# Order of the conditioning chain and of the ScalarE copies in an adaLN, attention and GRU kernel

## The chip, the cores and the metric

One core of one Trainium2 chip runs the whole kernel. The metric is device time in microseconds (us), from one launch. The kernel before takes 487.22 us, the median of three runs (486.86 to 487.56).

## The reference, cut to what matters

The input x is 128 batches x 32 positions x 256 features, float32; cond is 128 x 256. The program computes three things one after another:

```python
# 1. conditioning: block attention over 8 blocks of 4 positions
block_repr = x.reshape(B, 8, 4, H).sum(axis=2)
keys = block_repr @ Wk.T
keys = keys / sqrt(mean(keys**2) + EPS) * rms_weight
attn = softmax(keys @ q)                          # q = cond[1], 8 weights per batch
proj = (attn @ block_repr) @ Wo.T                 # one row per batch
y = layernorm(x + proj) * gamma + beta            # proj is spread over the 32 positions
# 2. causal attention, 32 heads of 8 features, 32 positions, with ALiBi
q, k, v = split(y @ W_attn + b_attn)
x = x + softmax(mask(q @ k.T / sqrt(8)) + alibi) @ v @ W_proj + b_proj
# 3. GRU over 32 time steps (state starts at cond), then a 256 x 256 linear layer
x = x + gru(cond, x) @ (weight * scale).T + bias
```

## The kernel before, in words

**Tiles and groups.** A tile is 128 tokens, that is 4 batches of 32 positions. Four tiles make a group of 16 batches; there are 8 groups and 32 tiles. The main loop runs over groups g and, within one, over steps i = 0 to 3 (`tile_step(g, i)`, with n = 4g + i). Each engine has its own `tile_step`, and the order of the calls in it, written out by hand, is the order of the work on that engine. Semaphores order the engines among each other; an engine that waits holds up all that stands behind it. After the groups the GRU runs, 32 steps one after another (lines 1311 to 1332); the change doesn't touch it.

**What a step does for attention.** TensorE (`tile_step` at L1202) computes the scores of tile n + 1 (L1115), transposes the attention output of tile n - 1 (L1149), transposes the probabilities of tile n (L1128), projects the output of tile n - 1 (L1157), and multiplies probabilities by values for tile n (`probs_v`, L1139). VectorE normalises (L805, L809), applies the mask (L784), takes the row maxima (L792), subtracts the maximum from the first half of the scores (L798) and adds the residual (L821). GpSimd (POOL) subtracts it from the second half (L469). ScalarE takes the exponentials (L561) and copies results out of PSUM: the transposed probabilities and attention output (both L491, as `copy_out`).

**What is done for the next group.** In step 0 TensorE transposes y of group g + 1 (`transpose_y`, L1055) into ps_a, once ScalarE's `cond_out` has emptied it (L1051). ScalarE's `transpose_out` (L527) reads each of the two feature halves twice: as yT_r[0], rounded to the fp32r format, and as yT in full. GpSimd's `rest_of_y` (L443) subtracts them, which gives the low part yT_r[1]. `work_ahead` on TensorE then computes q in step 0 and k in step 1 (both L1066) and v in step 2 (L1075), each product as high x high, low x high, high x low; ScalarE writes them out in `q_chunk`, `k_chunk`, `v_half`. SyncE moves k and v by DMA into block-diagonal tiles (`load_k` L332, `save_v` L336, `load_v` L342).

**The conditioning chain for group g + 2.** In step 3 of the group before, TensorE multiplies the block sums by Wk and Wo (`block_products`, L1013), and ScalarE copies the product to kw_sb (`cond_out`, by L491). Then, in step 0: VectorE `cond_sums` (L699, L701, L704), GpSimd `inverse_rms` (the power -1/2, L436), VectorE `cond_scores` (L708), TensorE `cond_row` (L1025: the column of scores is turned into a row in ps_o). In step 1: VectorE `cond_shift` (L716, L718), ScalarE `cond_exp` (L512), VectorE `cond_normalise` (L723 to L727), TensorE `cond_col` (L1030), VectorE `select_blocks` (L734), TensorE `batch_proj` (L1036), ScalarE `round_proj`, VectorE `rest_of_proj` (L740), TensorE `spread_proj` (L1042). In step 2 VectorE adds the projection to x (L750) and takes the statistics (L758, L766), from which GpSimd makes the inverse deviation; in step 3 ScalarE's `normalise_tokens` (L519) makes y. This chain exists for groups g + 2 < 8, that is in the steps of groups 0 to 5.

Of the kernel before, what the change touches and what calls it, by code (L numbers as in the profile page):

```python
# [8 lines left out]
ACT = mybir.ActivationFunctionType  # L9
# [10 lines left out]
C = E // P  # L20
# [3 lines left out]
NG = B // GB  # L24
NT = B // TB
# [55 lines left out]
def adaln_attn_gru_ffn(nc, x_tok, x_feat, cond_t, wkwo, wqkv, wp, wih, whh, wf, vecs, rows, consts, v_dram, out):  # L81
    ctx = ExitStack()
    with ctx:
# [41 lines left out]
        vec = sb("vec", [P, NVEC])  # L125
# [287 lines left out]
        def _(pool):  # L413
# [20 lines left out]
            def inverse_rms(k):  # L434
                pool.wait_ge(c_mean, k + 1)
                nc.gpsimd.tensor_tensor(rinv[:, :], rinv[:, :], minus_half[:, 0:1], ALU.pow).then_inc(c_pow, 1)  # L436
# [36 lines left out]
            for g in range(NG):  # L473
                for i in range(GT):
                    n = GT * g + i
                    if i == 0 and g + 1 < NG:
                        rest_of_y(g + 1)
                    if i == 0 and g + 2 < NG:
                        inverse_rms(g + 2)
                    if n + 1 < NT:  # L480
                        softmax_shift(n + 1)
                    if i == 1 and g + 3 < NG:
                        block_sums(g + 3)
                    if i == 2 and g + 2 < NG:
                        inverse_std(g + 2)
# [3 lines left out]
        def _(act):  # L489
# [29 lines left out]
                    nc.scalar.activation(y[:, i, :], y[:, i, :], ACT.Identity, bias=centre[:, i:i + 1],  # L519
                                         scale=rstd[:, i:i + 1]).then_inc(y_done, 1)  # L520

            def transpose_out(k):

                for c in range(C):
                    act.wait_ge(yt_mm, C * k + c + 1)
                    for dst, out_sem in ((yT_r[0], yt_hi), (yT, yt_out)):
                        nc.scalar.activation(dst[:, c, :], ps_a[:, c * 512:(c + 1) * 512], ACT.Identity,  # L527
                                             bias=vec[:, V_BETA + c:V_BETA + c + 1],
                                             scale=vec[:, V_GAMMA + c:V_GAMMA + c + 1]).then_inc(out_sem, 1)

            def q_chunk(k, m):

# [50 lines left out]
            cond_out(1, ps_m[:, :])  # L583
            normalise_tokens(0)
            act.wait_ge(l_small, 3 * DMA)
            transpose_out(0)
            act.wait_ge(w_ready, 1)
            q_chunk(0, 0)
            q_chunk(0, 1)
# [10 lines left out]
            def tile_step(g, i):  # L600

                n = GT * g + i
                last_group = g + 1 == NG
                if i == 0 and not last_group:
                    transpose_out(g + 1)
                if i == 1 and g + 2 < NG:
                    cond_exp(g + 2)
                if n > 0:
                    attn_out(n - 1)
                probs_out(n)  # L610
                if i == 0 and not last_group:
                    q_chunk(g + 1, 0)
                    q_chunk(g + 1, 1)
                if i == 1 and not last_group:
                    k_chunk(g + 1, 0)
                    k_chunk(g + 1, 1)
                if i == 1 and g + 2 < NG:
                    round_proj(g + 2)
                if i == 2 and not last_group:
                    v_half(g + 1, 0)  # L620
                    v_half(g + 1, 1)
                if i == 3 and g + 2 < NG:
                    normalise_tokens(g + 2)
                if n + 1 < NT:
                    softmax_exp(n + 1, (n + 1) % 2)
                if i == 3 and g + 3 < NG:
                    cond_out(g + 3, ps_a[:, 0:512])
                if g == NG - 2 and i <= C:
                    if i == 0:
                        act.wait_ge(wqkv_lo, 3)  # L630
                        act.wait_ge(w_ready, 2)
                    if i < C:
                        copy_out(w_ih_r[0][:, i, :], w_ih[:, i, :]).then_inc(w_hi, 1)
                    else:
                        copy_out(w_f_r[0][:, :, :], w_f[:, :, :]).then_inc(w_hi, 1)
# [43 lines left out]
        def _(dve):  # L679
# [200 lines left out]
            def tile_step(g, i):  # L880

                n = GT * g + i
                norm_ahead = g + 2 < NG
                if n > 0:
                    normalise(n - 1)
                if norm_ahead and i == 1:
                    cond_shift(g + 2)
                if norm_ahead and i == 2:
                    add_proj(g + 2)
                if n + 1 < NT:  # L890
                    softmax_mask(n + 1, (n + 1) % 2)
                if norm_ahead and i == 0:
                    cond_sums(g + 2)
                if norm_ahead and i == 1:
                    cond_normalise(g + 2)
                if norm_ahead and i == 2:
                    token_stats(g + 2)
                if n + 1 < NT:
                    softmax_max(n + 1, (n + 1) % 2)
                if norm_ahead and i == 1:  # L900
                    select_blocks(g + 2)
                if n + 1 < NT:
                    softmax_shift(n + 1, (n + 1) % 2)
                if norm_ahead and i == 2:
                    mean_and_variance(g + 2)
                if norm_ahead and i == 0:
                    cond_scores(g + 2)
                if g == NG - 2 and 0 < i:
                    rest_of_gru_weights(i - 1)
                if n > 0:  # L910
                    residual(n - 1, (n - 1) // GT, (n - 1) % GT)
                if norm_ahead and i == 1:
                    rest_of_proj(g + 2)
# [95 lines left out]
        def _(pe):  # L1009
# [192 lines left out]
            def tile_step(g, i):  # L1202

                n = GT * g + i
                last_group, norm_ahead = g + 1 == NG, g + 2 < NG
                if i == 0 and not last_group:
                    transpose_y(g + 1, norm_ahead)
                if n + 1 < NT:
                    scores(n + 1, (n + 1) // GT, (n + 1) % GT)
                if n > 0:  # L1210
                    transpose_attn(n - 1)
                transpose_probs(n, n % 2, first=(n == 0))
                if n > 0:
                    project_out(n - 1)
                if norm_ahead and i == 1:
                    cond_col(g + 2)
                if i < 3 and not last_group:
                    work_ahead(g + 1, i, 0)
                    work_ahead(g + 1, i, 1)
                if norm_ahead and i == 0:  # L1220
                    cond_row(g + 2)
                if g + 3 < NG and i == 3:
                    pe.wait_ge(v_out, 2 * g + 4)
                    block_products(g + 3, ps_a[:, 0:512])
                if norm_ahead and i == 1:
                    pe.wait_ge(k_out, 2 * g + 3)
                    batch_proj(g + 2)
                probs_v(n, g, i)
                if norm_ahead and i == 1:
                    pe.wait_ge(k_out, 2 * g + 4)  # L1230
                    spread_proj(g + 2)

            for g in range(NG):
                for i in range(GT):
# [158 lines left out]
```

## Time and profile before

| | |
|---|---|
| median of 3 runs | 487.22 us |
| profiled execution | 486.86 us |
| its span, first to last instruction | 485.1 us |
| TensorE (PE) busy | 438.2 us, 90% |
| VectorE (DVE) busy | 343.6 us, 71% |
| ScalarE (ACT) busy | 241.1 us, 50% |
| GpSimd (POOL) busy | 108.4 us, 22% |

The busy time is the sum of an engine's instructions over the whole span. An engine that is busy for a small share can still end a wait of another, so the table alone doesn't say what a change of order is worth. PEld is TensorE's loading of weights, which runs beside its products. In rows of the timeline the first number is the start in us from the span's start, the second the time that the instruction, or the run of them, took. Instructions of one engine overlap there by some hundredths of a microsecond.

### The profile page before, as it was taken

What the parts mean: (1) busy time and instruction counts of PE and PEld (TensorE: products, weight loads), DVE (VectorE), ACT (ScalarE), POOL (GpSimd) and SP (SyncE); (2) the same over time, 40 slices, a digit from 0 to 9 for tenths busy, and PEclk for the clock granted to TensorE, in tenths of its full rate; (3) what the DMA queues carried; (4) which work ended last, traced back from release to release, by engine and by line L of the source; (5) the groups of instructions that cost most, each with busy time, mean ns of one, the idle gap of its engine ahead of it and who ended that gap; (6) DMA issues with size and microseconds to landing.
All of it is one profiled execution on the core that took longest, in us unless ns stands there. A gap on an engine that the chain in (4) does not pass through costs nothing.

```text
span 485.1 us, 13494 instructions
## 1 busy us (share of the span) xinstructions
PE 438.2 (90%) x5458; PEld 359.0 (74%) x5458; DVE 343.6 (71%) x1015; ACT 241.1 (50%) x561; POOL 108.4 (22%) x119
## 2 busy tenths in 40 slices
PE   7679789899898998998989786999999999999995
PEld 5247467667676785776767675979998999899984
DVE  3815388789787987888888885366677767676665
ACT  1252545756648457466486454444444444444342
POOL 7330334443334445333251221000000000000000
PEclk9759899999999999999999999999999999999999
DMA  8511411332503314123130220000100001010101
GB/s 302 228 43 35 143 44 34 89 104 64 155 20 92 111 41 129 64 74 95 29 95 20 62 66 3 1 2 1 43 23 24 22 24 45 0 45 2 43 23 65
DMA packets 34268, 30.36 MB, mean 63 GB/s; under 512 B 4128, under 2 KB 29344, under 8 KB 34208
## 3 DMA queue, kind: packets, MB, share of 16 engines
q1 hardware_dynamic: 34208, 29.51, 19.1%
q8 instruction: 43, 0.70, 0.6%
q14 instruction: 17, 0.14, 0.1%
HBM read 16.91 MB, written 8.39 MB: 52 GB/s over the span
## 4 chain that ended last, share of the span: by engine, by line
PE 68%; DVE 14%; issue 7%; ACT 5%; SPq 3%; DMA 2%; POOL 1%; DVEq 0%; ACTq 0%; POOLq 0%
PE ps_a L1066 7%; PE ps_s L1271 6%; PE ps_t L1271 6%; PE ps_o L1271 6%; PE ps_s L1243 5%; PE ps_s L1115 5%; PE ps_t L1243 4%; PE ps_a L1075 4%; PE ps_a L1243 4%; PE ps_m L1243 3%; PE ps_m L1157 3%; PE ps_o L1139 3%; PE ps_t L1128 3%; SPq L332 2%; PE ps_a L1013 2%
## 5 line engine op out<-in xcount | busy, mean ns | idle before, releaser
L469 POOL TENSOR_TENSOR sc<-masked,mx 128x512 f32<-128x512 f32 x32 | 46.2, 1445 | 123.8 <-DVE mx L792 123.8
L1066 PE MATMUL ps_a<-yT_r,w_qkv_r 128*128 128x512 f32 x192 | 51.5, 418 | 1.5 <-ACT yT_r L527 1.5
L784 DVE COPY_PREDICATED masked<-kst,ps_s 128x512 f32<-128x512 int32 x64 | 44.0, 734 | 9.7 <-PE ps_s L1115 6.3
L1066 PEld LDWEIGHTS ps_a<-yT_r,w_qkv_r 128*128 128x128 f32 x192 | 36.5, 198 | 10.4 <-issue 2.1
L561 ACT ACTIVATE sc<-sc 128x512 f32<-128x512 f32 x64 | 37.1, 622 | 7.6 <-DVE sc L798 6.2
L792 DVE TENSOR_REDUCE mx<-masked 128x16 f32<-128x512 f32 x64 | 40.4, 672 | 0.0
L647 ACT ACTIVATE zg<-ps_t,brz 128x128 f32<-128x128 f32 x64 | 20.0, 364 | 38.8 <-PE ps_t L1271 38.8
L929 DVE SCALAR_TENSOR_TENSOR rg<-ps_o,vec,rg 128x128 f32<-128x128 f32 x64 | 19.5, 346 | 27.3 <-PE ps_o L1271 23.4
L1157 PE MATMUL ps_m<-oT,w_p 128*128 128x128 f32 x256 | 35.4, 282 | 3.6 <-ACT oT L491 3.6
L491 ACT ACTIVATE pT<-ps_t 128x512 f32<-128x512 f32 x64 | 35.0, 599 | 4.2 <-PE ps_t L1128 3.5
L1115 PE MATMUL ps_s<-kbd,qn 64*32 64x256 f32 x1024 | 35.9, 390 | 0.7 <-DMA kbd<-kn 0.7
L1128 PE MATMUL ps_t<-kst,sc 128*128 128x128 f32 x256 | 35.4, 282 | 1.1 <-issue 1.1
L1271 PEld LDWEIGHTS ps_s<-hT,w_hh 128*128 128x128 f32 x256 | 33.1, 191 | 4.5 <-DVE hT L947 2.4
L1157 PEld LDWEIGHTS ps_m<-oT,w_p 128*128 128x128 f32 x256 | 31.7, 195 | 5.4 <-ACT oT L491 5.3
L1271 PE MATMUL ps_s<-hT,w_hh 128*128 128x128 f32 x256 | 34.2, 276 | 0.9 <-DVE hT L947 0.6
L1271 PE MATMUL ps_o<-hT,w_hh 128*128 128x128 f32 x256 | 33.8, 275 | 0.0
L1271 PE MATMUL ps_t<-hT,w_hh 128*128 128x128 f32 x256 | 33.8, 275 | 0.0
L1128 PEld LDWEIGHTS ps_t<-kst,sc 128*128 128x128 f32 x256 | 30.5, 147 | 2.4 <-issue 2.4
L647 ACT ACTIVATE rg<-ps_s,brz 128x128 f32<-128x128 f32 x64 | 20.0, 363 | 24.3 <-PE ps_s L1271 24.3
L1271 PEld LDWEIGHTS ps_t<-hT,w_hh 128*128 128x128 f32 x256 | 31.2, 192 | 0.1
L1271 PEld LDWEIGHTS ps_o<-hT,w_hh 128*128 128x128 f32 x256 | 31.2, 192 | 0.0
L491 ACT ACTIVATE h_r<-hT 128x256 fp32r<-128x256 f32 x32 | 13.4, 418 | 35.7 <-DVE hT L947 35.7
(116 smaller groups left out, 872.8 us busy)
## 6 DMA issues: line engine op xcount, KB each, us to landing
xf<-in_x_feat SPq DMA_DIRECT2D x8, 512.0 KB, 4.2
xg<-in_x_tok SPq DMA_DIRECT2D x8, 512.0 KB, 5.0
kbd<-kn SPq DMA_DIRECT2D x128, 32.0 KB
v_dram<-vn SPq DMA_DIRECT2D x16, 256.0 KB, 2.5
vbd<-v_dram SPq DMA_DIRECT2D x64, 64.0 KB, 2.0
out_feat<-ost SPq DMA_DIRECT2D x16, 256.0 KB, 2.0
w_qkv<-in_wqkv SPq DMA_DIRECT2D x1, 768.0 KB, 7.5
w_ih<-in_wih SPq DMA_DIRECT2D x1, 768.0 KB, 10.2
```

Of the source, the lines that this page charges most:

```text
L469: nc.gpsimd.tensor_tensor(shifted, kept, m.unsqueeze(2).to_broadcast([P, NH // 2, S]), ALU.subtract).then_inc(sc_sub[1], 1)
L491: return nc.scalar.activation(dst, src, ACT.Copy)
L561: nc.scalar.activation(part, part, ACT.Exp).then_inc(sc_exp, 1)
L647: nc.scalar.activation(dst[:, c, :], gate_part(gate, c, t), ACT.Sigmoid, bias=brz[:, b0 + c:b0 + c + 1]).then_inc(done, 1)
L784: nc.vector.copy_predicated(kept, keep.unsqueeze(1).to_broadcast([P, NH // 2, S]), ps_s[:, h * 512:(h + 1) * 512].rearrange("p (h k) -> p ...
L792: nc.vector.tensor_reduce(m, kept, axis=AX_X, op=ALU.max).then_inc(sc_max, 1)
L1066: last = nc.tensor.matmul(bank, w_qkv_r[a][:, c, first_col + m * P:first_col + (m + 1) * P], yT_r[b][:, c, :], start=(a == b == c == 0), s ...
L1115: last = nc.tensor.matmul(ps_s[b * S:(b + 1) * S, out_cols], qn[rows, g % 2, c, cols], kbd[rows, c, :, cols], start=True, stop=True, tile_ ...
L1128: last = nc.tensor.transpose(ps_t[:, col:col + P], sc[:, p, col:col + P], ident)
L1157: last = nc.tensor.matmul(ps_m[:, E + m * P:E + (m + 1) * P], w_p[:, c, m * P:(m + 1) * P], oT[:, c, :], start=(c == 0), stop=(c == C - 1))
L1243: last = nc.tensor.matmul(dst, w_r[a][:, c, col:col + P], rhs_r[b][:, c, :], start=first, stop=(c == C - 1 and a == 1), skip_group_check=True)
L1271: last = nc.tensor.matmul(dst, w_hh[:, c, col + m * P:col + (m + 1) * P], old[:, c, :], start=(which is None and c == 0 and m == 0), stop= ...
```

## The change

It reorders calls in the four `tile_step`s; no instruction is added or taken away except waits. GpSimd: `inverse_rms` goes ahead of `rest_of_y`. ScalarE: `transpose_out` is cut into its four copies, and the last of them goes behind `attn_out`; `cond_exp` moves from the beginning of step 1 to between the two copies of q in step 0; `cond_out` goes ahead of the exponentials of step 3. VectorE: in step 0, `cond_sums` goes ahead of the mask, `cond_scores` directly behind it, and `cond_shift` comes from step 1 to behind the subtraction of the maximum; in step 1, `cond_normalise` goes ahead of the mask and `select_blocks` ahead of the maxima. TensorE: `cond_row` goes ahead of the q products, `cond_col` ahead of the transposes of the probabilities; `probs_v` of step 0 now first waits for `c_sub`; `spread_proj` is written at the beginning of step 2 instead of the end of step 1.

```diff
--- before.py
+++ after.py
@@ -473,10 +473,10 @@
             for g in range(NG):
                 for i in range(GT):
                     n = GT * g + i
+                    if i == 0 and g + 2 < NG:
+                        inverse_rms(g + 2)
                     if i == 0 and g + 1 < NG:
                         rest_of_y(g + 1)
-                    if i == 0 and g + 2 < NG:
-                        inverse_rms(g + 2)
                     if n + 1 < NT:
                         softmax_shift(n + 1)
                     if i == 1 and g + 3 < NG:
@@ -519,14 +519,12 @@
                     nc.scalar.activation(y[:, i, :], y[:, i, :], ACT.Identity, bias=centre[:, i:i + 1],
                                          scale=rstd[:, i:i + 1]).then_inc(y_done, 1)
 
-            def transpose_out(k):
-
-                for c in range(C):
-                    act.wait_ge(yt_mm, C * k + c + 1)
-                    for dst, out_sem in ((yT_r[0], yt_hi), (yT, yt_out)):
-                        nc.scalar.activation(dst[:, c, :], ps_a[:, c * 512:(c + 1) * 512], ACT.Identity,
-                                             bias=vec[:, V_BETA + c:V_BETA + c + 1],
-                                             scale=vec[:, V_GAMMA + c:V_GAMMA + c + 1]).then_inc(out_sem, 1)
+            def transpose_out(k, c, dst, out_sem):
+
+                act.wait_ge(yt_mm, C * k + c + 1)
+                nc.scalar.activation(dst[:, c, :], ps_a[:, c * 512:(c + 1) * 512], ACT.Identity,
+                                     bias=vec[:, V_BETA + c:V_BETA + c + 1],
+                                     scale=vec[:, V_GAMMA + c:V_GAMMA + c + 1]).then_inc(out_sem, 1)
 
             def q_chunk(k, m):
 
@@ -583,7 +581,9 @@
             cond_out(1, ps_m[:, :])
             normalise_tokens(0)
             act.wait_ge(l_small, 3 * DMA)
-            transpose_out(0)
+            for c in range(C):
+                transpose_out(0, c, yT_r[0], yt_hi)
+                transpose_out(0, c, yT, yt_out)
             act.wait_ge(w_ready, 1)
             q_chunk(0, 0)
             q_chunk(0, 1)
@@ -602,14 +602,19 @@
                 n = GT * g + i
                 last_group = g + 1 == NG
                 if i == 0 and not last_group:
-                    transpose_out(g + 1)
-                if i == 1 and g + 2 < NG:
-                    cond_exp(g + 2)
+                    transpose_out(g + 1, 0, yT_r[0], yt_hi)
+                    transpose_out(g + 1, 0, yT, yt_out)
+                    transpose_out(g + 1, 1, yT_r[0], yt_hi)
                 if n > 0:
                     attn_out(n - 1)
+                if i == 0 and not last_group:
+                    transpose_out(g + 1, 1, yT, yt_out)
                 probs_out(n)
                 if i == 0 and not last_group:
                     q_chunk(g + 1, 0)
+                if i == 0 and g + 2 < NG:
+                    cond_exp(g + 2)
+                if i == 0 and not last_group:
                     q_chunk(g + 1, 1)
                 if i == 1 and not last_group:
                     k_chunk(g + 1, 0)
@@ -621,10 +626,10 @@
                     v_half(g + 1, 1)
                 if i == 3 and g + 2 < NG:
                     normalise_tokens(g + 2)
+                if i == 3 and g + 3 < NG:
+                    cond_out(g + 3, ps_a[:, 0:512])
                 if n + 1 < NT:
                     softmax_exp(n + 1, (n + 1) % 2)
-                if i == 3 and g + 3 < NG:
-                    cond_out(g + 3, ps_a[:, 0:512])
                 if g == NG - 2 and i <= C:
                     if i == 0:
                         act.wait_ge(wqkv_lo, 3)
@@ -883,28 +888,27 @@
                 norm_ahead = g + 2 < NG
                 if n > 0:
                     normalise(n - 1)
+                if norm_ahead and i == 0:
+                    cond_sums(g + 2)
                 if norm_ahead and i == 1:
-                    cond_shift(g + 2)
+                    cond_normalise(g + 2)
                 if norm_ahead and i == 2:
                     add_proj(g + 2)
                 if n + 1 < NT:
                     softmax_mask(n + 1, (n + 1) % 2)
                 if norm_ahead and i == 0:
-                    cond_sums(g + 2)
+                    cond_scores(g + 2)
                 if norm_ahead and i == 1:
-                    cond_normalise(g + 2)
+                    select_blocks(g + 2)
                 if norm_ahead and i == 2:
                     token_stats(g + 2)
                 if n + 1 < NT:
                     softmax_max(n + 1, (n + 1) % 2)
-                if norm_ahead and i == 1:
-                    select_blocks(g + 2)
-                if n + 1 < NT:
                     softmax_shift(n + 1, (n + 1) % 2)
+                if norm_ahead and i == 0:
+                    cond_shift(g + 2)
                 if norm_ahead and i == 2:
                     mean_and_variance(g + 2)
-                if norm_ahead and i == 0:
-                    cond_scores(g + 2)
                 if g == NG - 2 and 0 < i:
                     rest_of_gru_weights(i - 1)
                 if n > 0:
@@ -1205,30 +1209,32 @@
                 last_group, norm_ahead = g + 1 == NG, g + 2 < NG
                 if i == 0 and not last_group:
                     transpose_y(g + 1, norm_ahead)
+                if norm_ahead and i == 2:
+                    pe.wait_ge(k_out, 2 * g + 4)
+                    spread_proj(g + 2)
                 if n + 1 < NT:
                     scores(n + 1, (n + 1) // GT, (n + 1) % GT)
                 if n > 0:
                     transpose_attn(n - 1)
+                if norm_ahead and i == 1:
+                    cond_col(g + 2)
                 transpose_probs(n, n % 2, first=(n == 0))
                 if n > 0:
                     project_out(n - 1)
-                if norm_ahead and i == 1:
-                    cond_col(g + 2)
+                if norm_ahead and i == 0:
+                    cond_row(g + 2)
                 if i < 3 and not last_group:
                     work_ahead(g + 1, i, 0)
                     work_ahead(g + 1, i, 1)
-                if norm_ahead and i == 0:
-                    cond_row(g + 2)
                 if g + 3 < NG and i == 3:
                     pe.wait_ge(v_out, 2 * g + 4)
                     block_products(g + 3, ps_a[:, 0:512])
                 if norm_ahead and i == 1:
                     pe.wait_ge(k_out, 2 * g + 3)
                     batch_proj(g + 2)
+                if norm_ahead and i == 0:
+                    pe.wait_ge(c_sub, g + 3)
                 probs_v(n, g, i)
-                if norm_ahead and i == 1:
-                    pe.wait_ge(k_out, 2 * g + 4)
-                    spread_proj(g + 2)
 
             for g in range(NG):
                 for i in range(GT):
```

## Rows read from the trace of the kernel before

**Rows 1.** The page's first line.

```profile
span 485.1 us, 13494 instructions
```

**Rows 2.** Windows: stretch, its length, each engine's busy time (instructions), clock, DMA share, GB/s.

```profile
153.96:185.71 31.75, 29.24 (x526) 22.57 (x527) 25.79 (x68) 19.53 (x37) 12.93 (x15) 1.00 0.28 86
```

**Rows 3.** Timeline of TensorE in one group: start, time, instruction, [idle before <-releaser].

```profile
153.96 1.06 PE L1055 MATMUL ps_a<-kst,y 128*128 128x128 f32 x8 [0.92 <-issue]
...
157.74 1.16 PE L1157 MATMUL ps_m<-oT,w_p 128*128 128x128 f32 x8 [0.44 <-ACT oT L491]
158.65 3.05 PE L1066 MATMUL ps_a<-yT_r,w_qkv_r 128*128 128x512 f32 x12
162.26 0.38 PE L1025 MATMUL ps_o<-kst,cs 128*1 128x128 f32 x2 [0.56 <-DVE cs L708]
162.37 0.88 PE L1139 MATMUL ps_o<-vbd,pT 128*32 128x40 f32 x64
...
166.72 0.38 PE L1030 MATMUL ps_o<-kst,cT 1*128 1x1 f32 x2 [0.29 <-DVE cT L727]
...
179.03 1.12 PE L1115 MATMUL ps_s<-kbd,qn 64*32 64x256 f32 x32
```

**Rows 4.** Waits of TensorE, 56 to 250 us: total us, times, longest.

```profile
PE ps_o L1025 <- DVE cs L708: 3.2, 6, 0.6
PE ps_m L1157 <- ACT oT L491: 2.2, 5, 0.4
```

**Rows 5.** Timeline of ScalarE around the start of that group.

```profile
150.26 2.07 ACT L519 ACTIVATE y<-y,centre,rstd 128x256 f32<-128x256 f32 x4
152.24 1.14 ACT L561 ACTIVATE sc<-sc 128x512 f32<-128x512 f32 x2
153.28 0.58 ACT L491 ACTIVATE kw_sb<-ps_a 128x512 f32<-128x512 f32 x1
154.62 0.78 ACT L527 ACTIVATE yT_r<-ps_a,vec 128x512 fp32r<-128x512 f32 x1 [0.76 <-PE ps_a L1055]
...
157.29 0.40 ACT L491 ACTIVATE oT<-ps_m 128x256 f32<-128x256 f32 x1
```

**Rows 6.** Timeline of VectorE in steps 0 and 1 of that group.

```profile
153.48 0.43 DVE L809 TENSOR_TENSOR on<-ps_o,rden 128x256 f32<-128x256 f32 x1
...
156.84 0.73 DVE L784 COPY_PREDICATED masked<-kst,ps_s 128x512 f32<-128x512 int32 x1
...
157.47 0.40 DVE L699 CUSTOM_DVE_ANT_0 junk<-kw_sb 128x256 f32<-128x256 f32 x1
...
157.80 1.50 DVE L701 CUSTOM_DVE_ANT_0 junk<-kw_sb,wqr 128x256 f32<-128x256 f32 x1
...
161.20 1.00 DVE L708 TENSOR_TENSOR cs<-dotq,rinv 128x1 f32<-128x1 f32 x1
...
164.34 0.28 DVE L718 TENSOR_TENSOR cT<-ps_o,cmx 1x128 f32<-1x128 f32 x1
```

**Rows 7.** Timeline of GpSimd in step 0 of that group.

```profile
156.21 2.81 POOL L443 TENSOR_TENSOR yT_r<-yT,yT_r 128x512 fp32r<-128x512 f32 x2 [3.68 <-ACT yT L527]
159.58 0.55 POOL L436 TENSOR_TENSOR rinv<-rinv,minus_half 128x1 f32<-128x1 f32 x1 [0.56 <-DVE rinv L704]
160.76 1.43 POOL L469 TENSOR_TENSOR sc<-masked,mx 128x512 f32<-128x512 f32 x1 [0.64 <-DVE mx L792]
```

**Rows 8.** Lines L701 and L708: shortest, median, longest in ns, of all eight.

```profile
L701 DVE CUSTOM_DVE_ANT_0 junk<-kw_sb,wqr x8: 420/1495/1514, 10.0 to 221.3; 128x256 f32<-128x256 f32 x8
...
L708 DVE TENSOR_TENSOR cs<-dotq,rinv x8: 159/1004/1006, 11.7 to 224.7; 128x1 f32<-128x1 f32 x8
```

**Rows 9.** Timeline of TensorE in groups 0 and 6.

```profile
66.01 0.38 PE L1025 MATMUL ps_o<-kst,cs 128*1 128x128 f32 x2 [0.41 <-DVE cs L708]
...
251.59 1.16 PE L1157 MATMUL ps_m<-oT,w_p 128*128 128x128 f32 x8 [0.95 <-ACT oT L491]
```

**Rows 10.** Timeline of SyncE's queue: the loads of k in that group.

```profile
170.85 11.03 SPq L332 DMA_DIRECT2D kbd<-kn  x16
```

## The prediction

> **What bounds the kernel now.** I read the time in windows first, then TensorE's gaps in one group, then what each of the engines that it waits for was doing just before.
>
> The span is 485.1 us [rows 1]; the profiled execution took 486.86 us, 1.76 more than its span, and lies 0.36 under the median of 487.22. The attention part is eight groups of four steps. In the group that begins at 153.96 the period is 31.75 us, of which TensorE is busy 29.24 at the full granted clock of 1.00 [rows 2]; the groups beginning at 90.41, 122.19 and 185.71 have the same period within 0.04. TensorE is the bound, and what can be won in a group is its idle 2.5 us. The timeline of TensorE [rows 3] shows where that idle time is: 0.92 before the transposes of y (153.96), 0.44 before the first output projection (157.74), 0.56 before the scores row (162.26), 0.29 before the weights column (166.72), and 0.29 more before the spread. The waits over the whole attention part [rows 4] show that this repeats: the scores row waited 6 times for 3.2 us, the projection 5 times for 2.2 us. The 0.92 stands at the start of groups 1 to 5, five times; group 0 starts with a wait of the prologue that the change doesn't touch, and groups 6 and 7 have no such conditioning product ahead.
>
> Who ends each gap: the 0.92 ends when ScalarE has copied kw_sb at 153.28 to 153.86, and ScalarE did both exponentials (152.24, 1.14 us for two) ahead of it although block_products was done when normalise_tokens ended at 152.33 [rows 5]. The 0.44 ends with the oT copy at 157.29, which stood behind all four copies of transpose_out, 0.67 us each [rows 5]. The 0.56 ends with `cond_scores` on VectorE (161.20, 1.00 us) [rows 6].
>
> **Part 1: cond_out ahead of softmax_exp (ScalarE, step 3).** The copy (0.58) now runs from 152.33 to 152.91. probs_v ends 0.92 before 153.96, at 153.04, so the transposes start there: 0.92 gone, the cover of the copy being probs_v itself. The two exponentials end 0.58 later, at 153.96 for their old 153.38. Their reader, transpose_probs, comes over 2 us later. The first yT_r copy started 0.66 after the first transpose [rows 3, 5], which would be 153.70; the exponentials hold it until about 153.86. That 0.16 is carried below.
>
> **Part 2: oT copy ahead of the last yT copy (ScalarE, step 0).** From 153.86, three copies of 0.67 end at 155.87; oT then starts, and the projection follows its start by 0.45 (157.29 to 157.74), so at 156.32. TensorE reaches the projection 3.34 after the transposes began (153.96 to 157.30), at 156.38. No gap is left: 0.44 gone, with 0.06 to spare. The last yT copy moves behind oT and ends near 156.85; it is late only for `rest_of_y`.
>
> **Part 3: the conditioning chain in step 0 (VectorE, GpSimd, TensorE).** VectorE ends normalise at 153.91 and then waited for the scores until 156.19, so cond_sums fits into idle time. It took long before: `junk` of L701 1.50 us, against 0.42 in group 0 [rows 6, 8]. The long one began at 157.80, while GpSimd ran `rest_of_y` (156.21 to 159.02) and ended 0.28 after that did [rows 7]. At the new place GpSimd is idle, since inverse_rms now stands ahead of rest_of_y in its queue. I take 0.42. The bounds are 0.42 and 1.50. So cond_sums runs from 153.91: 0.33 for L699 (157.47 to 157.80), 0.42 for L701, and the power starts 0.28 after L701 (159.30 to 159.58), at about 154.95, and ends 0.55 later at 155.5. GpSimd's rest_of_y for c=0 then starts at 155.5 instead of 155.3: 1.3 to 1.4 us each (2.81 for two), end 156.85; that for c=1 needs the late yT copy and runs 156.95 to 158.35.
>
> The masks follow the scores, 0.92 earlier than before: they end at 157.47 − 0.92 = 156.55. cond_scores is then next. It reads two SBUF operands, cost 0.16 alone and 1.00 beside GpSimd's softmax_shift, which ended at 162.19 while cond_scores ended at 162.20 [rows 6, 7, 8]. Now rest_of_y of c=0 holds it up to 156.85; it ends at about 157.0. TensorE ends the projection 0.91 after 156.38, at 157.27 to 157.3 (157.74 to 158.65, [rows 3]), and so finds cond_row's operand ready: the 0.56 is gone, with 0.3 to spare. Bounds on cond_scores' end: 156.7 (nobody in the way) and 158.4 (it waits out both halves of rest_of_y). I take 157.0: L699 came in just between those two halves at 157.47 and delayed the second, so a waiting VectorE is served at a handover [rows 6, 7].
>
> The Trainium skill has a rule that speaks against this place (SBUF — State Buffer, Who interferes with whom): a VectorE instruction with two SBUF inputs contends with a GpSimd instruction that reads SBUF, and the later of the two blocks fully. By that rule the trace agrees (1.50 against 0.42, 1.00 against 0.16), and it also says that the change brings rest_of_y over both cond_scores and softmax_shift. By the row that costs TensorE nothing; if the rule's block lasts through both halves, it is rival B.
>
> cond_row takes 0.34 and its work is only moved. The twelve products of work_ahead (3.05 us) begin at 157.6; the first four, 1.0 us, need no low part of yT_r, and rest_of_y is ready at 158.35 for the fifth at 158.6. Spare: 0.25.
>
> The new wait on c_sub before probs_v: cond_shift stands behind the two reductions and VectorE's shift. From L701's end to L708's start there were 1.9 us, of which these three are 1.8. From 157.0 that is 158.8; the shift too reads two SBUF operands and may be held by rest_of_y until 158.35, so 159.0. cond_shift is two instructions of 0.28 [rows 6]: c_sub at 159.6. TensorE comes to probs_v at 157.6 + 3.0 = 160.6. Spare 1.0; behind the wait would stand probs_v, the next scores, and with them VectorE's normalise. Bounds: 0 and, if every handover goes to GpSimd, about 0.4. cond_exp between the two q_chunk copies finds c_sub there (q_chunk 0 ends near 159.8) and costs ScalarE 0.3 in idle time.
>
> **Part 4: step 1.** VectorE does normalise (0.8) and then cond_normalise, three instructions near 0.28 each, so c_wt comes 0.05 + 0.8 + 0.85 = 1.7 after probs_v's end. cond_col now stands behind scores and transpose_attn only, about 1.4 (3.34 less 1.06 for the y transposes and 0.9 for those of the probabilities). That leaves 0.3 of idle time, in place of the 0.29 of before: gain zero, bounds −0.1 and +0.1. select_blocks, ahead of the maxima, is far ahead of batch_proj. "Spread to the third step" moves nothing on TensorE: between probs_v of step 1 and the scores of step 2 nothing else stands, so the instruction order is the same as before, with its waits. Its 0.29 stays.
>
> The K loads are tied to kn, and so is everything up to step 3's scores, which ran at 179.03 without a gap, 8.2 us after the loads began at 170.85 [rows 3, 10]. All that is shortened lies ahead of kn. No DMA is issued from ScalarE, VectorE or GpSimd, so nothing is moved past one.
>
> **Groups 0 and 6.** Group 0 had 0.41 before cond_row [rows 9]; rest_of_y ends at about the time of the masks there, so I count 0.2. Group 6 had 0.95 before the projection, behind four copies; one copy less gives 0.66.
>
> **Sum.** 5 × (0.92 + 0.44 + 0.56) = 9.6; plus 0.2 and 0.66: 10.5 us. From 486.86 that is 476.4, and from the median 476.7. I give 476.5.
>
> **The rivals.**
> B: cond_scores waits out both halves of rest_of_y. Its end is 158.4 instead of 157.0, TensorE stalls 158.45 − 157.3 = 1.15 before cond_row, five times: 10.5 − 5.8 = 4.7, about 482. For it: in before the long cases ended exactly with GpSimd's. Against: L699's place between the halves.
> C: one of the small margins (0.06, 0.25, 0.3) fails by some tenths, for example because yT's last copy and with it rest_of_y is late: 0.3 to 0.6 back per group, about 479.
> D, slower: the masks themselves are held by rest_of_y, as their flag operand lies in SBUF. Then masks start only at 158.4, end at 159.7, and cond_row's operand comes at 159.9: a stall of 2.6 in each of five groups against 1.92 won, 3.4 lost, less 0.66 in group 6: about 490. It decides from a delay of 1.92 on. Against: in before the masks ran at 156.84 beside rest_of_y (156.21) in 0.73 [rows 6, 7].
> E: the gaps vanish and come back before the next wait (nothing gained, 487): for it only the two gaps of 0.29 that stay; against, no computing engine but TensorE is within 5 us of the period (ScalarE and VectorE are busy 19.5 and 25.8 of 31.75 [rows 2]).
>
> **Chances.** Forecast 0.74, C 0.10, B 0.10, D 0.03, E 0.03. The forecast's own bounds: step 1's ±0.5 in all, group 0's ±0.4, run to run 0.4, so 475.3 to 477.8. The range for 8 in 10 takes in C and leaves out B, D and E: 474.8 to 480. Measurement can tell about 0.2% (1 us) here: faster 0.94, same 0.03, slower 0.03.
>
> **What would show it.** Right: groups of about 29.8 us; no gap before the y transposes, before the first projection and before the scores row; the second `junk` instruction at 0.42; L708 of 0.3 to 0.5; a gap of 0.2 to 0.3 before the weights column, and 0.29 before the spread. Wrong: a gap of over 1 us before the scores row with L708 at over 1.5 us (B); masks that end more than 1.4 after the scores (D); a gap inside the q products for yT_r's low part (C); a gap before probs_v of step 0 that ends with c_sub; a later K load at step 3.

## The result and the profile after

The changed kernel takes 475.6 us, the median of four runs (472.97 to 477.77), beside 487.04 of four runs of the kernel before; the ratio is 0.9766, 95% interval 0.9734 to 0.9798, so 11.4 us or 2.3% faster. A second measurement with six runs gave 475.34 and a ratio of 0.9763 (0.9739 to 0.9788). The profiled execution took 476.0 us, its span is 474.2.

The group that answers to [rows 2], in the same view:

```profile
148.24:178.31 30.07, 29.43 (x527) 22.47 (x527) 24.26 (x68) 19.63 (x38) 12.64 (x15) 1.00 0.31 90
```

The period fell from 31.75 to 30.07, TensorE's idle time from 2.5 us to 0.64. VectorE is busy for 1.5 us less although it does the same work: the second `junk` instruction took 1.50 us and takes 0.42, cond_scores 1.00 and now 0.21, the shift 0.68 and now 1.01. The time for which such an instruction is held up beside one of GpSimd's counts as busy. TensorE in this group, for [rows 3]:

```profile
147.43 0.80 PE L1143 MATMUL ps_o<-vbd,pT 128*32 128x40 f32 x64
148.24 1.06 PE L1059 MATMUL ps_a<-kst,y 128*128 128x128 f32 x8
...
151.50 1.16 PE L1161 MATMUL ps_m<-oT,w_p 128*128 128x128 f32 x8
152.59 0.38 PE L1029 MATMUL ps_o<-kst,cs 128*1 128x128 f32 x2
152.90 3.06 PE L1070 MATMUL ps_a<-yT_r,w_qkv_r 128*128 128x512 f32 x12
155.90 0.80 PE L1143 MATMUL ps_o<-vbd,pT 128*32 128x40 f32 x64
...
158.50 0.38 PE L1034 MATMUL ps_o<-kst,cT 1*128 1x1 f32 x2 [0.33 <-DVE cT L732]
```

Three of the four brackets of [rows 3] are gone: the y transposes follow probs_v within 0.01, projection and scores row have no wait. The weights column has one of 0.33, and the spread (165.17), which is not in [rows 3], one of 0.29 as before.

ScalarE, for [rows 5]: kw_sb is now ahead of the exponentials, and oT (151.06) ahead of the second yT copy.

```profile
147.53 0.61 ACT L491 ACTIVATE kw_sb<-ps_a 128x512 f32<-128x512 f32 x1
148.04 1.13 ACT L559 ACTIVATE sc<-sc 128x512 f32<-128x512 f32 x2
...
151.06 0.39 ACT L491 ACTIVATE oT<-ps_m 128x256 f32<-128x256 f32 x1
151.32 0.80 ACT L525 ACTIVATE yT<-ps_a,vec 128x512 f32<-128x512 f32 x1
```

VectorE and GpSimd, for [rows 6, 7]:

```profile
149.35 0.42 DVE L706 CUSTOM_DVE_ANT_0 junk<-kw_sb,wqr 128x256 f32<-128x256 f32 x1
...
150.05 0.55 POOL L436 TENSOR_TENSOR rinv<-rinv,minus_half 128x1 f32<-128x1 f32 x1 [2.22 <-DVE rinv L709]
...
150.65 1.30 POOL L443 TENSOR_TENSOR yT_r<-yT,yT_r 128x512 fp32r<-128x512 f32 x1
...
151.13 0.72 DVE L789 COPY_PREDICATED masked<-kst,ps_s 128x512 f32<-128x512 int32 x1
...
151.76 0.21 DVE L713 TENSOR_TENSOR cs<-dotq,rinv 128x1 f32<-128x1 f32 x1
...
152.26 1.28 POOL L443 TENSOR_TENSOR yT_r<-yT,yT_r 128x512 fp32r<-128x512 f32 x1 [0.31 <-ACT yT L525]
...
153.09 1.01 DVE L803 TENSOR_TENSOR sc<-masked,mx 128x512 f32<-128x512 f32 x1
...
154.32 0.28 DVE L723 TENSOR_TENSOR cT<-ps_o,cmx 1x128 f32<-1x128 f32 x1
```

The second `junk` instruction takes 0.42 us, cond_scores 0.21. The mask ran beside rest_of_y in 0.72, unhindered. The shift L803 took 1.01 instead of 0.68: it waited for the second half of rest_of_y, and nobody waited for it.

**Where the 10.9 us of the two spans are.** The starts of the y transposes cut both traces into groups; the last mark is the load of the sigmoid table by which the GRU begins on ScalarE.

| stretch | before | after | less | forecast |
|---|---|---|---|---|
| up to group 0 | 57.06 | 57.00 | 0.06 | 0 |
| group 0 | 33.35 | 31.26 | 2.09 | 1.12 |
| groups 1 to 4 | 127.09 | 119.92 | 7.17 | 7.68 |
| group 5 | 28.97 | 28.07 | 0.90 | 1.00 |
| groups 6, 7 | 58.09 | 57.40 | 0.69 | 0.66 |
| GRU | 180.54 | 180.55 | -0.01 | 0 |

The forecast column is the prediction's sum, sorted by these marks. A gap before the y transposes of a group stands at the end of the stretch of the group before it. So group 0 has 0.92 and the 0.2 of the scores row, groups 1 to 4 have 1.92 each, and group 5 has 0.44 + 0.56.

### The profile page after: what moved, and what is told of

The parts are those of the page before. It is cut to its first block, busy times and chain, and to the rows that moved or that the text cites. A ratio compares the mean times of both kernels' runs of the same rounds, so it can differ in the third digit from the quotient of the medians.

```text
span 474.2 us, 13494 instructions
## 1 busy us (share of the span) xinstructions
PE 438.6 (92%) x5458; PEld 357.6 (75%) x5458; DVE 334.8 (71%) x1015; ACT 241.8 (51%) x561; POOL 106.9 (23%) x119
## 4 chain that ended last, share of the span: by engine, by line
PE 79%; DVE 8%; ACT 4%; issue 3%; SPq 3%; DMA 2%; POOL 1%; DVEq 0%; ACTq 0%; POOLq 0%
PE ps_a L1070 10%; PE ps_s L1277 6%; PE ps_t L1277 6%; PE ps_o L1277 6%; PE ps_m L1161 5%; PE ps_t L1132 5%; PE ps_s L1249 5%; PE ps_s L1119 5%; PE ps_t L1249 4%; PE ps_a L1079 4%; PE ps_a L1249 4%; PE ps_m L1249 4%; PE ps_o L1143 3%; PE ps_a L1017 3%; SPq L332 2%
## 5 line engine op out<-in xcount | busy, mean ns | idle before, releaser
L1143 PEld LDWEIGHTS ps_o<-vbd,pT 128*32 128x32 f32 x2048 | 21.9, 111 | 11.9 <-issue 9.1
```

## The experiments

Each kernel was built from the one before or the changed one by the edit shown. Besides the medians I compare the period of the groups 1 to 4 in the traces, as the medians carry more noise: the runs of one kernel spread over 1.6 to 5.8 us. "Changed" is the changed kernel.

| kernel | median us | ratio to before (95%) | mean period, groups 1 to 4 | less |
|---|---|---|---|---|
| before | 486.13 to 487.22 | | 31.77 | |
| cond_out ahead only | 485.36, again 483.03 | 0.9959 (0.9933-0.9986), 0.9943 (0.9919-0.9966) | 30.88, 30.90 | 0.89 |
| oT ahead only | 482.62 | 0.9917 (0.9885-0.9950) | 30.98 | 0.79 |
| both of these | 480.98 | 0.9876 (0.9845-0.9906) | 30.18 | 1.59 |
| chain only | 482.99 | 0.9914 (0.9879-0.9948) | 31.35 | 0.42 |
| changed, again | 475.34 | 0.9763 (0.9739-0.9788) | 29.99 | 1.78 |
| changed, GpSimd's order undone | 486.38 | 0.9979 (0.9955-1.0002) | 31.62 | 0.15 |
| before, GpSimd's order swapped | 502.87 | 1.0303 (1.0258-1.0349) | 33.94 | -2.17 |
| changed, cond_col later | 473.10, again 473.52 | 0.9686 (0.9650-0.9722), 0.9725 (0.9699-0.9752) | 29.61, 29.64 | 2.15 |
| also spread later | 475.95 | 0.9748 (0.9713-0.9782) | 29.84 | 1.93 |
| also mask ahead of add_proj | 472.18 | 0.9709 (0.9682-0.9737) | 29.47 | 2.30 |

**1. cond_out ahead of the exponentials, alone, and once more.**

```diff
+                if i == 3 and g + 3 < NG:
+                    cond_out(g + 3, ps_a[:, 0:512])
                 if n + 1 < NT:
                     softmax_exp(n + 1, (n + 1) % 2)
-                if i == 3 and g + 3 < NG:
-                    cond_out(g + 3, ps_a[:, 0:512])
```

> The kernel before with one edit: the copy of kw_sb ahead of the two exponentials in step 3. My theory: the gap of 0.92 us before the y transposes goes, five times, 4.6 us in all, about 482.5; the exponentials end 0.58 later, so the projection's gap grows from 0.44 to about 0.6 and the one before the scores row shrinks by the same. The 1.14 us stall of TensorE in group 0 (at 69.65 in the trace of before) stays, if it belongs to the instruction stream, which is unchanged here. Rival (what is won comes back at the next wait): no more than 1 us.

> The kernel before with cond_out ahead of the exponentials, once more: its first trace had periods of 30.9 us for 31.77 (4.4 us in five groups), but its median was only 2 us under that of before. Theory (the period is the truth, the median was raised by stalls that fall at random): periods of 30.9 again and 3.5 to 4.5 us less. Rival (most executions of it are slower than the traced one): 1.5 to 2.5 us less again, and in this trace a stall or a longer wait in some group.

The mechanism is as expected, in both traces: no wait at the y transposes, 0.60 at the projection for 0.44, 0.47 at the scores row for 0.56, and 0.89 us less per group. It also settles who ended the 0.92: the profile of before names no releaser for it in five of six cases (`<-issue`), and it goes when ScalarE's copy comes earlier. The medians fell by only 2.0 and 2.8 us (by the ratios), not by 4.6 or by the 3.5 to 4.5 of the second theory. The second trace, of the slowest of twelve executions, shows one reason, a stall of TensorE in group 5 for which the profile names no other engine (timeline of TensorE):

```profile
225.52 0.27 PE L1149 MATMUL ps_m<-kst,on 128*128 128x128 f32 x1 [2.60 <-issue]
```

It stands between two transposes of which the second has no wait in the program. Behind it the granted clock was 0.62 from 225.5 to 229.0, and the eight products of the projection took 1.91 us for 1.06. The first trace, of the second fastest execution, has a stall of 1.52 at the same instruction and no drop of the clock behind it; its group 5 took 30.48 us, that of the second trace 32.98. So the stalls are real, but these two don't fall at random places, as the second theory had it. The stall of group 0, which the first expectation let stand, is missing in the first trace and is there with 0.94 in the second. What the untraced executions lost can't be read.

**2. oT ahead of the last yT copy, alone.**

```diff
                 if n > 0:
                     attn_out(n - 1)
+                if i == 0 and not last_group:
+                    transpose_out(g + 1, 1, yT, yt_out)
                 probs_out(n)
```

> The kernel before with one edit: transpose_out cut up, the oT copy ahead of the last yT copy. My theory: in groups 0 to 5 it gives nothing alone, since cond_row still waits for VectorE's chain, which starts from the scores and doesn't move; the gap of 0.44 goes and the one before cond_row grows from 0.56 to 1.0. Only group 6 wins, 0.66 us: about 486.5. Rival (the gaps are independent): 5 x 0.44 + 0.66 = 2.9 us, about 484.2.

Missed: 4.0 us by the ratio instead of 0.7, 0.79 per group instead of nothing. The rival was nearer but for a reason that it didn't have. The timeline of one group:

```profile
156.10 0.42 DVE L705 CUSTOM_DVE_ANT_0 junk<-kw_sb,wqr 128x256 f32<-128x256 f32 x1
156.12 1.56 POOL L443 TENSOR_TENSOR yT_r<-yT,yT_r 128x512 fp32r<-128x512 f32 x1 [0.31 <-ACT yT L525]
...
157.74 2.12 PE L1070 MATMUL ps_a<-yT_r,w_qkv_r 128*128 128x512 f32 x8 [0.29 <-POOL yT_r L443]
```

The later yT copy makes the second half of rest_of_y come 0.02 us after VectorE's instruction (L705 here, L701 in before); in before it came 0.25 us ahead of it (157.55). Now GpSimd waits (1.56 us; the first half takes 1.30) and VectorE doesn't (0.42 for 1.50), so the scores are ready earlier and the gap before cond_row is gone as well; in its place TensorE waits 0.29 us for rest_of_y. The order in which the two instructions began decided 1.08 us of VectorE's time.

**3. Both edits on ScalarE.**

> The kernel before with both edits on ScalarE alone (cond_out ahead of the exponentials, oT ahead of the last yT copy), no change to the conditioning chain. My theory: 4.6 + 0.66 = 5.3 us, about 481.8: the gap before cond_row grows to about 1.0. Rival (gaps independent): 7.5 us, about 479.6.

The period fell by 1.59, the sum of the two alone less 0.09; the ratio gives 6.0 us, nearer my 5.3 than the rival's 7.5, but my reason (the gap before cond_row grows to 1.0) was wrong: in groups 1 to 5 that gap is gone, and by the periods the rival's 1.36 per group was the nearer. What is left of the gaps is 0.19 before the fifth q product. This trace has a stall without a releaser too, 1.20 us at 220.25.

**4. The conditioning chain alone.** The changed kernel with both of its edits on ScalarE's copies undone, as in the diffs of 1 and 2.

> The changed kernel with both edits of its copies undone (transpose_out whole, cond_out behind the exponentials), so only the conditioning chain's move on VectorE, GpSimd and TensorE, with cond_exp in step 0. My theory: only the gap of 0.56 before the scores row goes (five times, and 0.41 in group 0), less about 0.25 per group that cond_row now costs between dense products; the 0.92 and the 0.44 stay. That is 1.5 to 2.5 us, and 1.1 more if the stall of group 0 is gone here as it is in the changed kernel: about 484. Rival (the chain's move is the main part of the gain): over 5 us, under 482.

The gap before the scores row is gone, 0.92 and 0.44 stay, 0.42 us per group: as expected in the trace, and the rival's 5 us are not reached. The ratio gives 4.2 us, above my 1.5 to 2.5; 482.99 is 1 us under my 484 with the stall gone. Its span is 3.1 us shorter, although its prologue ended 0.9 later.

**5. GpSimd's order in the changed kernel, undone.**

```diff
-                    if i == 0 and g + 2 < NG:
-                        inverse_rms(g + 2)
                     if i == 0 and g + 1 < NG:
                         rest_of_y(g + 1)
+                    if i == 0 and g + 2 < NG:
+                        inverse_rms(g + 2)
```

> The changed kernel with one thing undone: on GpSimd rest_of_y is again ahead of inverse_rms. My theory: rest_of_y of c=1 ends about 5.3 us after the y transposes begin, the power 0.6 later, cond_scores then at about 6.1, while TensorE is ready for cond_row at 4.4: a gap of about 1.7 us in groups 1 to 5 and about 0.5 in group 0, 9 us in all, about 484.5. Rival (the order on GpSimd is hidden, since there is 1 us of slack before probs_v): no difference from the changed kernel, 475.5.

```profile
158.27 0.38 PE L1029 MATMUL ps_o<-kst,cs 128*1 128x128 f32 x2 [1.62 <-DVE cs L713]
```

Five gaps of 1.61 to 1.63 us, and 0.38 in group 0: the theory, within 0.12. The median, 486.38, is 1.9 above my 484.5. With two calls swapped back on an engine that is busy for 22% of the time nearly the whole gain is lost: 0.9979, and 0.9766 with them in the new order. That is not their share of the gain, as experiment 3 has 0.9876 with the old order of GpSimd and of the whole chain: in the new order of the other engines the swap is a condition.

**6. The same swap in the kernel before.** There inverse_rms goes ahead of rest_of_y, and nothing else is changed.

> The kernel before with only GpSimd's order changed: inverse_rms ahead of rest_of_y. My theory: L701 drops from 1.50 to 0.42 us, since no rest_of_y runs beside it, and the gap before cond_row goes; but rest_of_y now waits for the means, ends 2 us later than the fifth q product needs it (2.6 to 3 in group 0), so the net is a loss of about 1.5 us per group: +10 us, about 497. Rival (the shorter L701 is what counts): 0.56 per group won, about 484.

```profile
135.70 2.13 PE L1066 MATMUL ps_a<-yT_r,w_qkv_r 128*128 128x512 f32 x8 [2.18 <-POOL yT_r L443]
```

Slower by 3.0%, where I had said 10 us. Gaps of 2.18 to 2.21 us in groups 1 to 5 and 3.03 in group 0 for the low part of yT_r, and none before cond_row, as forecast. A normal period is 33.6, 1.8 more than before, where I had said 1.5. Group 3 had 34.94, with eight q products lasting 3.58 for 2.13 at a granted clock of 0.57 (169.3 to 173.0), and in group 0 they took 3.42 behind the gap of 3.03, at 0.58 (67.2 to 70.7). Such drops are a part of the loss that my sum didn't have. The same swap is a loss of 1.8 us per group in the kernel before, where cond_sums stands behind the mask, and a gain of 1.6 in the changed kernel, where it stands ahead.

**7. cond_col behind the transposes of the probabilities.**

```diff
-                if norm_ahead and i == 1:
-                    cond_col(g + 2)
                 transpose_probs(n, n % 2, first=(n == 0))
+                if norm_ahead and i == 1:
+                    cond_col(g + 2)
```

> The changed kernel with cond_col behind the transposes of the probabilities, ahead of the projection. My theory: the gap of 0.33 before the weights column goes, six times, since the 0.9 us of transposes covers it: 1.9 us less than the changed kernel, about 473.7. Rival (cond_col's wait only moves, or select_blocks now holds up VectorE's maxima): no difference, 475.6, or more.

> The changed kernel with cond_col behind the transposes of the probabilities, once more and now beside the changed kernel on the same chip. Theory: period 29.6 for 30.0, 2 us less than the changed kernel. Rival (the first difference of 2.5 was the chip's): within 0.5 us of it.

Both traces have no wait before cond_col, and the period is 0.35 to 0.37 shorter. On one chip with the changed kernel: 473.52 against 475.34, 0.9725 (0.9699-0.9752) against 0.9763 (0.9739-0.9788). The intervals overlap, so the 1.8 us rest on the two measurements and the two traces together.

**8. The spread behind the scores of step 2, and then the mask ahead of add_proj.**

```diff
-                if norm_ahead and i == 2:
-                    pe.wait_ge(k_out, 2 * g + 4)
-                    spread_proj(g + 2)
                 if n + 1 < NT:
                     scores(n + 1, (n + 1) // GT, (n + 1) % GT)
+                if norm_ahead and i == 2:
+                    pe.wait_ge(k_out, 2 * g + 4)
+                    spread_proj(g + 2)
```

> The changed kernel with cond_col behind the transposes of the probabilities, and spread_proj behind the scores of step 2. My theory: both small gaps go, 0.33 and 0.29, six times: 3.7 us less than the changed kernel, about 472; VectorE's add_proj starts 1.0 later, and the masks, maxima and shift of step 2 behind it, which ScalarE's exponentials have about 1 us of slack for. Rival (that slack is not there, y of the next group is late): the second move gives its 1.7 back at step 3 or at the next y transposes, 473.7 or more.

The rival held. VectorE waited for the spread, and its normalise of step 3 came late (timelines of VectorE and TensorE):

```profile
194.18 1.29 DVE L755 TENSOR_TENSOR y<-xg,ps_a 128x512 f32<-128x512 f32 x2 [0.56 <-PE ps_a L1046]
```

```profile
201.58 0.44 PE L1153 MATMUL ps_m<-kst,on 128*128 128x128 f32 x2 [0.69 <-DVE on L814]
```

0.29 won, 0.69 lost: the period rose from 29.61 to 29.84. The next kernel has the mask in the idle time:

```diff
-                if norm_ahead and i == 2:
-                    add_proj(g + 2)
                 if n + 1 < NT:
                     softmax_mask(n + 1, (n + 1) % 2)
+                if norm_ahead and i == 2:
+                    add_proj(g + 2)
```

> The changed kernel with cond_col behind the transposes of the probabilities, spread_proj behind the scores of step 2, and VectorE's mask of step 2 ahead of add_proj. With the spread moved alone, VectorE sat idle 0.56 us for it, was 0.5 us late at the end of step 2, and TensorE lost 0.7 at the output transposes of step 3. Theory: the mask fills that idle time, so the 0.7 goes and the 0.29 before the spread is won: period 29.3, about 3.5 to 4 us less than the changed kernel. Rival (add_proj now lies late enough to hold project_v, or the statistics and with them y come late): period 29.6 or more.

The 0.69 shrank to 0.29 (at 201.01), the period to 29.47, between theory and rival. This is the fastest kernel of the study, 472.18 us, but the interval doesn't part it from the one without its last two edits (473.52).

**9. The changed kernel again.**

> The changed kernel itself, beside the kernels of this call. If the ledger of group periods holds (1.8 us per group, five groups, 0.9 to 2 in group 0, 0.9 in group 5, 0.7 in group 6), its time is 10.5 to 11.5 us under the kernel before. If a stall of TensorE in group 0 of the one trace of before (1.14 us) was chance and not part of the kernel, this trace of the changed kernel may have such a stall elsewhere or none, and the difference of medians stays near 10.5.

475.34 us, 10.8 under the 486.13 of before; periods of 30.02, 30.10, 29.98 and 29.87, and no stall without a releaser.

## Why the prediction was right

The forecast was 476.5 us, 10.5 less than before; measured are 475.6, inside its range, and 11.4 less; between the two traces it is 10.9. The gaps went as worked out; that the total came so close is in part luck, as the misses below cancel. By its own steps:

- **The bound.** TensorE's idle time in a group was what could be won, and was what was won: [rows 3] against the rows after. The instructions are the same, and the GRU is unchanged to 0.01 us.
- **Part 1, 0.92.** Right in place and size: 0.89 alone, in two traces.
- **Part 2, 0.44.** The gap went as worked out (oT's start 2.82 after the first transpose, forecast 2.83). The step "it is late only for `rest_of_y`" was incomplete: in experiment 2 the lateness also freed VectorE's L701, and alone the edit is worth 0.79, not 0.44; in group 6 it cost time (below).
- **Part 3, 0.56.** The gap went and the margins held. From the first transpose, cond_scores ended after 3.73 us (forecast 3.96) and TensorE came to cond_row at 4.35 (forecast 4.25); c_sub after 6.36 with probs_v at 7.66 (forecast 6.56 and 7.56). But as a part of the gain the chain's move is worth 0.42 per group alone and 0.20 on top of the two copies (30.18 to 29.98). The step that was wrong is "cond_row takes 0.34 and its work is only moved": cond_row between dense products costs TensorE more than before probs_v. From its start to the next instruction's it is 0.31 now (152.59 to 152.90) and was 0.11 [rows 3], and the projection ahead of it takes 1.09 to the next start for 0.91. Of that 0.38, 0.13 is given back by a probs_v of 0.73 for 0.81 and q products of 3.00 for 3.05. The 0.25 that is left is what this group lacks: it gained 1.68 for 1.92. The other three of groups 1 to 4 gained 1.78, 1.79 and 1.92, mean of the four 1.79; why they lost less was not followed up.
- **Part 4, nothing.** Right: 0.33 before the weights column for a forecast of 0.3, 0.29 before the spread. Experiment 7 shows that the 0.33 was cond_col's place and could be had.
- **Group 0** gave 2.09 for 1.12, and this is the most mis-sized term. The trace of before has a stall of 1.14 us at 69.65 in it, which my sum let stand and which the changed kernel doesn't have; the gap of 0.41 before the scores row went whole, for 0.2; and cond_row's 0.38 goes off. That the stall was in the one trace and not in the other made up for what groups 1 to 5 lacked (0.61): luck, as far as the forecast goes.
- **Group 6** is right by luck too. The gap before the projection fell from 0.95 to 0.28, the forecast 0.66. But the late yT copy made the second half of rest_of_y end at 242.76, and the fifth q product, the first that needs the low part of yT_r, waited for it: the twelve take 3.33 us for 3.04 in before. TensorE's load of weights for it (242.82) waited 0.46 us for rest_of_y. Timeline of TensorE and GpSimd, after:

```profile
241.46 1.30 POOL L443 TENSOR_TENSOR yT_r<-yT,yT_r 128x512 fp32r<-128x512 f32 x1 [0.33 <-ACT yT L525]
241.62 3.33 PE L1070 MATMUL ps_a<-yT_r,w_qkv_r 128*128 128x512 f32 x12
```

Up to the next probs_v group 6 gained 0.38. The other 0.31 of the 0.69 came behind it, where the two traces have different waits for DMA (0.70 and 0.39 us before, 0.99 after), which the change doesn't touch. The nine traces of kernels with the moved oT copy all have 3.32 or 3.33 there, the five without it 3.04 or 3.05.
- **The rivals.** B (cond_scores waits out both halves of rest_of_y) didn't come: the first half ended at 151.95 and cond_scores at 151.97, and the second half waited 0.31 us for its yT copy. So whether VectorE would get in between two halves that follow each other directly, my argument against B, wasn't put to the test. L803 met the second half instead, at no cost. D (the masks are held) is ruled out by masks of 0.72 and 0.75 beside rest_of_y; all 64 of the trace lie between 0.71 and 0.75. C (a small margin fails) came in group 6 only; in groups 1 to 5 its margins (0.06, 0.25, 0.3) held, but experiments 2 and 3, with rest_of_y at 0.29 and 0.19 too late, show how thin the second is. E (the gaps come back at the next wait) is out, with 7.17 of 7.68 us won in groups 1 to 4.

The rule that the prediction took from the Trainium skill (SBUF — State Buffer, Who interferes with whom) agrees with the runs: the same L701 takes 0.42 or 1.50 us, and in experiment 2 it is rest_of_y that takes 1.56 for 1.30, as whoever is second waits.

**What stays open.** The stalls of TensorE without a releaser, 0.94 to 2.60 us, each inside a loop that has no wait. In groups 0 to 5, four of the six traces of kernels with the old order of cond_row and cond_col have one or two (before, both of experiment 1, experiment 3); none of the eight traces with the new order has. In group 7, where the order is the same in all, the kernel of experiment 5 has one of 0.75. So it may be that TensorE's order plays a part and that the gain has 1 us in it that no gap in [rows 3] explains, but this is not shown, and what the stalls are was not tested. Between experiment 3 (0.9876) and the changed kernel (0.9766) lie 5.4 us, of which the periods of groups 1 to 5 give 1; in the traces, which are 4.1 apart, experiment 3's stall of 1.20 in group 5 and 1.76 in groups 6 and 7 are most of the rest. These last two groups have a noise of their own, 56.84 to 59.51 us over the fourteen traces: the same kernel took 58.29 and 59.27 in experiment 1, 57.96 and 56.84 in experiment 7.

## What to carry to other kernels

Take the gaps of the bounding engine one by one, find the call that ends each, and look whether that call stands behind one whose reader comes later; the two moved copies alone gave 1.59 us per group, all edits together 1.79. When VectorE and GpSimd instructions both read two operands from SBUF, their order of arrival is part of the schedule: check the spread between shortest and longest of the same instruction, and who ran beside the long ones. A swap on a nearly idle engine can't be priced by itself: the same two calls exchanged lost 3% in the kernel before, and the changed kernel needs them exchanged. A copy that is moved back is late for its own reader: look at each group's version of it, as the one that fits in groups 1 to 5 cost 0.29 in group 6.

## What the runs showed of the hardware

- VectorE's multiply-and-sum of 128x256 with two SBUF operands: 0.42 us, or 1.50 when a GpSimd subtraction of 128x512 began just before it; GpSimd's subtraction 1.27 to 1.30 alone, 1.56 when it was second.
- A VectorE instruction that is held up beside GpSimd's counts as busy for all of that time: VectorE's busy time in the whole profile fell from 343.6 to 334.8 us with the same instructions.
- The masks, predicated copies of 128x512 from PSUM, were not held up by a GpSimd subtraction that ran beside them: 0.71 to 0.75 us in all 64.
- In group 0 the granted clock was 0.50, the lower of TensorE's two levels (1.2 GHz), from 57 to 60 us in the traces of before and changed, and 1.00 in both of cond_out alone (experiment 1), where eight y transposes took 1.06 us instead of 1.94. TensorE had been idle for 3.40 us in all of them. Little of it reached the time: in those two traces TensorE then waited 1.06 us for rest_of_y and 1.05 for the scores row. The group took 30.87 us in the first of them, and in before, less its stall and the gap of 0.92, 31.29.
- The same idle time doesn't always bring the clock down: in experiment 6 TensorE was idle for 2.18 to 2.21 us in each of groups 1 to 5, and eight q products then took 3.58 us at 0.57 in group 3 and 2.12 or 2.13 at 1.00 in the others.
